# Four waits of a fused attention, FFN and mixture-of-experts kernel moved; pair rows laid side by side and the final sums dealt one block later

## The reference, cut to what matters

```python
def _L0_xattn_ref(inputs_q, inputs_kv, Wq, bq, Wk, bk, Wv, bv, Wo, bo):   # H, HD = 16, 64
    q = einsum('bqm,mhd->bqhd', inputs_q, Wq) + bq
    k = einsum('bkm,mhd->bkhd', inputs_kv, Wk) + bk
    v = einsum('bkm,mhd->bkhd', inputs_kv, Wv) + bv
    attn = softmax(einsum('bqhd,bkhd->bhqk', q / sqrt(HD), k))
    return einsum('bqhd,hdm->bqm', einsum('bhqk,bkhd->bqhd', attn, v), Wo) + bo

def _dense_path(x, ...):                                                  # H, hd = 16, 16
    q, k, v = x @ wq, x @ wk, x @ wv
    attn = softmax(where(causal, q k^T / sqrt(hd), -inf))
    h = x + rmsnorm(attn v @ wo, attn_norm_w)
    ffn = silu(h @ w1) * (h @ w3) @ w2
    return h + rmsnorm(ffn, ff_norm_w)

def _sparse_path(x, router_w, ew1, ew2, ew3, moe_norm_w):                 # E = 8, K = 2
    topw, topi = top_k(softmax(x @ router_w), K)
    g = silu(x @ ew1[e]) * (x @ ew3[e]);  eo = g @ ew2[e]
    return rmsnorm(sum_k topw_k * eo[topi_k], moe_norm_w)

x = x + _L0_xattn_ref(layernorm(x), ctx_1024, ...)
y = layernorm(x);  x = x + _dense_path(y, ...) + _sparse_path(y, ...)
```

## Time and profile before

| | |
|---|---|
| median of 3 runs | 1634.62 us (1632.85 to 1635.26) |
| the profiled execution, its own time | 1636.36 us |
| its span in the trace | 1634.6 us |
| PE busy | 1439.1 us, 88% |
| DVE busy | 820.4 us, 50% |
| ACT busy | 572.3 us, 35% |
| POOL busy | 468.3 us, 29% |
| PE clock granted, mean | 0.953 |

### The profile page before, as it was taken

The page is one execution under the profiler, slowest core; times in us unless marked ns, Lnnn a source line. Parts: engine busy times, 40 slices in busy tenths (PEclk is TensorE's granted clock), DMA queues, the critical chain, the costliest instruction groups (busy, mean ns, idle before and its releaser), DMA issues.

```text
span 1634.6 us, 23062 instructions
## 1 busy us (share of the span) xinstructions
PE 1439.1 (88%) x7753; PEld 945.7 (58%) x7754; DVE 820.4 (50%) x1711; ACT 572.3 (35%) x1217; POOL 468.3 (29%) x663
## 2 busy tenths in 40 slices
PE   6887998899889987998799879988998879999976
PEld 6533566566665655566556655665565435666654
DVE  2626445743674357436643664365536713333448
ACT  2231543054215421541155115512540343333345
POOL 4312113131412132213222222322231114555533
PEclk9988899999999999999999999999999889999988
DMA  5063006000600060006000600160014423432254
GB/s 194 1 193 130 1 1 148 21 14 1 161 8 14 5 158 20 1 13 156 15 1 26 142 15 1 37 131 15 1 47 96 134 81 117 122 100 87 86 194 141
DMA packets 92314, 115.62 MB, mean 71 GB/s; under 512 B 24872, under 2 KB 66368, under 8 KB 92224
## 3 DMA queue, kind: packets, MB, share of 16 engines
q1 hardware_dynamic: 76480, 79.78, 17.5%
q10 hardware_dynamic: 9216, 16.78, 4.4%
q0 software_dynamic: 6528, 17.87, 3.1%
HBM read 70.31 MB, written 43.68 MB: 70 GB/s over the span
## 4 chain that ended last, share of the span: by engine, by line
PE 66%; DVE 12%; DMA 7%; issue 4%; ACT 4%; POOL 4%; ACTq 1%; SPq 1%; POOLq 0%; DVEq 0%
PE ps L1037 8%; PE ps L857 7%; PE ps L876 7%; DMA room<-parts_d 6%; PE ps L1001 6%; PE ps L961 5%; DVE nm L1483 4%; PE ps L947 4%; PE ps L1054 4%; PE ps L924 3%; PE ps L1011 3%; PE ps L890 2%; PE ps L813 2%; PE ps L846 2%; PE ps L981 2%
## 5 line engine op out<-in xcount | busy, mean ns | idle before, releaser
L1483 DVE TENSOR_REDUCE nm<-ps 128x2 f32<-128x256 f32 (+3 forms) x256 | 202.7, 821 | 104.5 <-PE ps L925 103.4
L1177 ACT ACTIVATE room<-ps 128x512 f32<-128x512 f32 x320 | 181.2, 598 | 163.0 <-PE ps L949 162.1
L1001 PE MATMUL ps<-hT,w 128*128 128x512 f32 x768 | 216.6, 427 | 0.0
L1011 PE MATMUL ps<-w,room 128*128 128x256 f32 x512 | 142.9, 411 | 34.5 <-DVE room L1532 34.5
L1001 PEld LDWEIGHTS ps<-hT,w 128*128 128x128 f32 x768 | 147.6, 200 | 34.6 <-DVE hT L1511 2.0
L924 PE MATMUL ps<-room 96*128 96x128 bf16 (+3 forms) x512 | 127.6, 311 | 45.0 <-DVE nm L1483 16.3
L1201 ACT ACTIVATE room<-ps 128x512 f32<-128x512 f32 x64 | 37.5, 597 | 339.0 <-PE ps L1001 339.0
L1037 PE MATMUL ps<-room 128*128 x288 | 139.0, 605 | 1.7 <-ACT room L1231 1.7
L947 PE MATMUL ps<-room 99*128 99x384 bf16 (+3 forms) x512 | 130.6, 313 | 6.5 <-ACT room L1177 5.5
L876 PE MATMUL ps<-room 128*128 128x256 f32 x512 | 124.9, 388 | 1.9 <-ACT room L1138 1.8
L1011 PEld LDWEIGHTS ps<-w,room 128*128 128x128 f32 x512 | 94.2, 201 | 54.0 <-DVE room L1532 40.1
(11 more groups left out here) (231 smaller groups left out, 2441.0 us busy)
## 6 DMA issues: line engine op xcount, KB each, us to landing
room<-parts_d SPq DMA_DIRECT2D x48, 256.0 KB, 8.3
room<-parts_d ACTq DMA_DIRECT2D x48, 256.0 KB, 9.2
room<-xs_d SPq DMA_DIRECT2D x72, 128.5 KB, 2.1
parts_d<-room SPq DMA_DIRECT2D x64, 128.0 KB, 1.8
room<-pair_d SPq DMA_DIRECT2D x8, 1024.0 KB, 7.2
room<-in_L_ffn_ew SPq DMA_DIRECT2D x24, 256.0 KB, 5.0
xin<-in_x SPq DMA_DIRECT2D x8, 512.0 KB, 9.7
parts_d<-xnT SPq DMA_DIRECT2D x32, 128.0 KB, 1.8
```

Source lines behind the costliest of these rows:

```text
L1001: last = mm(bank(up_banks(b, m)[i]), w[:, x, k, m * P:(m + 1) * P], hT[:, y, k, :], start=((x, y, k) == terms[0]), stop=((x, y, k) == term ...
L1011: last = mm(bank((6, 7)[half], D, t % 2 * D), gT[:, m % 2, t * P:(t + 1) * P], w2[:, m, :], start=(m == 0 and t % 2 == 0), stop=(m == FB - ...
L1177: done(fn(prob[:, u * 512:(u + 1) * 512], bank(6 + n % 2), ACT.Exp), "b_exp")
L1483: done(v.tensor_reduce(nm[:, t, 2 * hp:2 * hp + 2], pair_ps, AX.X, ALU.max, negate=True), "a_max")
```

## The change

- **Bias copy.** From walk 1 on POOL makes the `bq_bc` of the next batch in a new step `nx_bq`, one block of the FFN before the end of the walk. The copies for batches 0 and 1 stay in `x_turn`.
- **Key products by halves.** m 0 and m 1 wait for 31 of the 32 maxima, m 2 and m 3 for all.
- **q loads.** ACT issues the six loads of `rep_q` at the head of its step `v` (0), ahead of the copy for the scatter; there it waits for the six stores of the queries.
- **First shifts.** PE's `shift` (0) moves from block 6's start, ahead of `max` 16, to behind `max` 19; it waits until `max` 18 is reduced, and `max` 20 instead of `max` 16 waits for `mT`. `nx_stats` moves from the end of block 5 to that of block 6 and `nx_apply` from the end of block 6 to that of block 7.
- **Pair rows.** The row of token (b, t, p) and choice k in `pair_d` becomes ((b·128 + p)·4 + t)·2 + k. A partition of a pair load then reads 8 KB in a row instead of four pieces of 2 KB.
- **Final sums.** In `ending()` the `gate` and `mix` of a batch come one FFN block later than before, behind the `fd` steps, and `mix_sq` and `mix_y` two blocks after the gate's own number.

```diff
 for _m in range(3, FB):
-    STEPS += [("fu", _m, 0)] + ([("shift", 0)] if _m == 6 else []) + _max[:1] + [("fg", _m, 0), ("fu", _m, 1)] + _max[1:2]
-    STEPS += [("fg", _m, 1), ("fd", _m - 1, 0)] + _max[2:4] + [("fd", _m - 1, 1)] + _max[4:(5 if _m < 5 else 6)]
-    STEPS += {5: [("shift_parts", 0), ("nx_stats",)], 6: [("nx_apply",)]}.get(_m, [])
+    STEPS += [("fu", _m, 0)] + _max[:1] + [("fg", _m, 0), ("fu", _m, 1)] + _max[1:2]
+    STEPS += [("fg", _m, 1), ("fd", _m - 1, 0)] + _max[2:4] + ([("shift", 0)] if _m == 6 else []) + [("fd", _m - 1, 1)] + _max[4:(5 if _m < 5 else 6)]
+    STEPS += {5: [("shift_parts", 0)], 6: [("nx_stats",)], 7: [("nx_bq",), ("nx_apply",)]}.get(_m, [])
     _max = _max[(5 if _m < 5 else 6):]
...
 def ending():
     for m in range(FB + 1):
         if m < FB:
-            order += [("fu", m, 0), ("fu", m, 1), ("gate", m), ("mix", m), ("fg", m, 0), ("fg", m, 1)]
-        if m:
-            order += [("fd", m - 1, 0), ("fd", m - 1, 1), ("mix_sq", m - 1), ("mix_y", m - 1)]
+            order += [("fu", m, 0), ("fu", m, 1), ("fg", m, 0), ("fg", m, 1)]
+        if m >= 1:
+            order += [("fd", m - 1, 0), ("fd", m - 1, 1), ("gate", m - 1), ("mix", m - 1)]
+        if m >= 2:
+            order += [("mix_sq", m - 2), ("mix_y", m - 2)]
+    order += [("mix_sq", B - 1), ("mix_y", B - 1)]
...
-            pairs_v = pair_d[0:2 * B * S, :].rearrange("(b t p k) d -> b p t (k d)", b=B, t=T, k=2)
+            pairs_v = pair_d[0:2 * B * S, :].rearrange("(b p t k) d -> b p t (k d)", b=B, t=T, k=2)
...
-                                              (E + 1, [[P, E + 1]], 2 * B * S, 1), (2 * B * T, [[2 * P, B * T], [1, 2]], 0, 2)):
+                                              (E + 1, [[P, E + 1]], 2 * B * S, 1), (2 * B * T, [[2 * S, B], [2, T], [1, 2]], 0, 2 * T)):
...
-                    elif step[0] == "x_turn":
+                    elif step[0] == "x_turn" and (c is None or c == 0):
...
+                    elif step[0] == "nx_bq" and b > 0:
+                        need(pool, b, "pT_ps", 2 * T)
+                        need(pool, b, "scat", per["scat"])
+                        carry_wait(2)
+                        done(g.tensor_copy(bq_bc, bq[:, :].unsqueeze(2).to_broadcast([P, PAIRS, P])), "bq")
...
-                            if c is not None:
-                                need(pe, c, "a_max", per["a_max"])
+                        if c is not None and half == 0:
+                            need(pe, c, "a_max", per["a_max"] - 1 + k)
...
-                        if nmax == 16:
+                        if nmax == 20:
                             need(pe, b, "mT_sb", 1)
...
                         need(pe, (b, c)[i], "m_part", i + 1)
+                        if i == 0:
+                            need(pe, b, "a_max", 19)
...
                     elif kind == "v":
                         t = step[1]
                         if t == 0:
+                            if c is not None:
+                                need(act, c, "b_ps", per["b_ps"])
+                            need(act, b, "q_out", per["q_out"])
+                            for j in range(NREP):
+                                src = parts_d[Q_PART[j], 0, :, :, :].rearrange("(h d) a n -> d h (a n)", d=HD)
+                                done(act.dma_start(q_rep[j:KREP:NREP, :, :].rearrange("d (h a) n -> d h (a n)", a=KD), src), "rep_q", 16)
...
                         done(fn(g_b, g_a, ACT.Exp), "gexp")
-                        if c is not None:
-                            need(act, c, "b_ps", per["b_ps"])
-                        need(act, b, "q_out", per["q_out"])
-                        for j in range(NREP):
-                            src = parts_d[Q_PART[j], 0, :, :, :].rearrange("(h d) a n -> d h (a n)", d=HD)
-                            done(act.dma_start(q_rep[j:KREP:NREP, :, :].rearrange("d (h a) n -> d h (a n)", a=KD), src), "rep_q", 16)
```

## The result

| | before | after |
|---|---|---|
| median of 4 runs | 1634.94 us (1632.85 to 1641.13) | 1586.86 us (1586.43 to 1587.05) |
| ratio | | 0.9699, 95% interval 0.9673 to 0.9726 |
| span in the trace | 1634.6 us | 1584.7 us |
| PE clock granted, mean | 0.953 | 0.962 |

The account below looks back on a forecast made before the run. The prediction took PE's work plus its waits, and the slow clock behind them, to bound the kernel, with DVE deciding the maxima and ending. Terms -24.6 - 3.5 - 21.9 + 4.5 + 3.5 + 0 - 3.7 + 0 = -45.7 gave 1589 us, range 1574 to 1606.

Parts of the forecast that it names:

- the three waits of the earlier trace: PE's waits before the change: POOL's bias copy 14.7 us, query and key loads 13.8, DVE's copy to mT 12.7.
- First shifts, -28.1: Split to last maximum: DVE decides, its idle falls from 5.2 to 1.1 us; -24.6 in six walks, -3.5 in walk 7.
- Bias copy, -21.9: PE's bqk at walk starts: the 14.7 us wait for POOL goes, and -7.2 of slow clock behind it.
- Halves, +4.5: Key products: no earlier m 2, but PE's gaps merge to 1.8 us; clock falls in half of six walks, 1.5 us each.
- m 2 starts when it would have: Key products: x_turn's second half waits for DVE's bank 1 copy anyway, so starting m 0 and m 1 earlier gains 0.
- q loads, +3.5: FFN start to max 0: ACT held 4.4 us, tanh and data waits go; net +0.5 a walk, seven walks.
- the 21 that I had named as a sign of being wrong: Sign of error: max 0 over 21 us behind the first FFN matmul's old place.
- a rival at +3 a walk, with 0.22: The q loads cost what they hide: ACT's 4.4 us stay on the path, +21 instead of +3.5, 1606 us; chance 0.22.
- after every wait of over 2.5 us seen here: Premise for q loads: the clock falls again behind the 4.4 us wait, so the work ends at 1081.3, not 1079.5.
- my bound of 1.8: Key stores sharing DMA engines with the query loads would land up to 1.8 us later, holding the key loads behind them.
- Walk 0, ending, pair rows: Three terms: walk 0 at 0 (-3 to +4), ending -3.7 (-5.5 to 0), pair rows 0 (-2 to +2).
- Another wait takes its place: Rival: bqk starts early but PE then waits for exponentials or POOL's sums; half of 21.9 lost, 1600 us; chance 0.1.

Follow-up runs that it names:

- second trace of the changed kernel: The changed kernel without further edits, run in a second series on another chip; that series gave 0.9698 (0.9679 to 0.9717) against the kernel before.

## Why the prediction was right, and where it wasn't

The total was off by 2 us in the median, and by 4 between the two traces (-49.9 instead of -45.7 us). That it came so near is luck in part: the q loads cost 7 us more than forecast, and the stretch of the bias copy and the halves gave 10 us more, and the two nearly cancelled.

- **What bounds the kernel.** Right for two of the three waits of the earlier trace rows: those for POOL and for mT were on the path, and so was the clock behind them. The wait for data was on it too, but taken away alone it brought nothing (1.0012), since ACT's hold put another wait in its place.
- **First shifts, -28.1.** The table has -26.1. Undone alone it was 18.5, because the price holds a part that isn't fixed: 2.3 us a walk for the order and up to 1.6 for the clock. Right in its mechanism; that DVE decides fits its 18.68 us busy of 20.35 (I had 1.1 us idle, it is 1.7).
- **Bias copy, -21.9.** The mechanism was right, and undone alone it cost 22.7.
- **Halves, +4.5.** Wrong: the cost didn't come. The gap of 1.8 us did (0.44, then 1.64), but the clock behind it was 1.00 in walks 2 to 7 of the changed kernel. Beside the other changes it is even the old order that loses clock: with m 0 waiting for all maxima, 1.57 us in one piece, it fell in the same six walks, while in the kernel before it had been 1.00 there in walks 3 to 7. "m 2 starts when it would have" holds only as long as the clock stays up.
- **The two together.** The table's first row is -27.1 and not -17.4. Of the 9.7 us between them 4.5 are the term for the halves, 2.9 lie in walks 2 to 7 (24.8 us against the 21.9 of the bias copy), and 2.3 in walk 1, where the bias copy didn't move and for which I had nothing. What gave these 2.3 isn't shown; in the second trace of the changed kernel they are 1.2.
- **q loads, +3.5.** This step failed by its size. The hold of 4.4 us, the wait for hT and the end of the data's wait came as worked out; the clock behind the wait cost more than the 1.8 us that I took from the earlier trace rows, 2.9 us in the first 6.2 alone. Max 0 came 21.0 us behind the first FFN matmul's old place, just over the 21 that I had named as a sign of being wrong. The table has +10.3, undoing gives 11. I had weighed this as a rival at +3 a walk, with 0.22. It was that rival's mechanism at half its price, with the gain of the clock elsewhere hiding it in the total. My premise that the clock falls "after every wait of over 2.5 us seen here" was a misreading: the wait of 2.57 us for the first tanh of walk 7 (1229.91) left it at 1.00. Behind the 4.4 us for hT it was 0.50 in all seven walks. The Trainium skill says in TensorE: Matmul & The Clock Gate, section What's actually happening, that the slow clock is the default which activity releases; these seven rows agree with it.
- **Later key stores.** SP issued its key loads 1.4 us after the end of its last store before the change (1063.23 in walk 6), and 5.6 us after it in the changed kernel (1031.94). SP's wait in between is for the landing of the stores. That is 4.2 us more, and more than twice my bound of 1.8. It cost nothing here, since max 0 waits for the row numbers (0.38 us) and no longer for the data. The Trainium skill says in DMA: Bandwidth & Descriptors, section Queues, rings and completion order, that a DMA engine takes turns between the queues that have work; the trace agrees in the direction, stores beside loads of another queue land later.
- **Walk 0, ending, pair rows.** Walk 0 has -1.3 for 0, and the second trace of the changed kernel +0.8, so it is none. From the last maximum of walk 7 on it is -5.7 for -3.7: 3.4 behind the first gate, 0.9 between the last scatter and that gate (0.5 to 0.7 of it by the pair rows undone), 1.4 ahead of them.
- **"Another wait takes its place".** It did, but for the q loads and not for the bias copy.

The effects of undoing each edit alone add up to 22.7 + 18.5 + 1 + 1 + 4.4 - 11 = 37 us, and the change brought 49. Each has an uncertainty of some 4 to 6 us, and the falls of the clock don't add (in walks 1 to 6 the wait for mT lost clock five times before the change, three times with the shifts back, never with the q loads alone). How much of the 12 us is the one and how much the other stays open.

## What to carry to other kernels

Six loads issued in a row held ACT's work behind them for 3.87 us here, 0.64 us each; issued where ACT stood idle anyway, they cost it nothing. So put a DMA's issue where the engine would stand anyway, and deal a batch of loads to several such places rather than move it in one piece. When a wait for data is removed by starting the transfer earlier, count what the issuing engine then does late, and for whom. A wait of PE costs itself and what the clock loses behind it, and the second part can differ from walk to walk with the same wait, so single undone edits need not sum to the whole. A total that doesn't change can hide two stretches that do, as with the halves: compare the traces by stretches before an edit is taken to be worth nothing.

## What the runs showed of the hardware

- **The clock behind a wait isn't set by the wait alone.** In the 3 us behind it: after 4.3 to 4.4 us for hT 0.50 in all seven walks of the changed kernel; after 3.4 to 5.1 us for data 0.50 in all seven with the loads on SP; after 2.57 to 3.25 us with the loads back 0.66 to 0.70. But 1.57 us ahead of m 0 brought 0.52 to 0.58 in six walks with the halves back, where 1.72 us at that place in the kernel before had left 1.00 at the start of walks 3 to 7; in the run with the loads dealt out 2.32 and 2.36 us left it at 1.00 and 2.19 us brought 0.54; and the same 1.72 us for mT left 1.00 in one walk and 0.50 to 0.71 in five of the kernel before, 1.00 in all six with the q loads alone.
- **An issue of a DMA can lie beside the engine's own copy**: 1001.38 to 1002.00 beside 1001.42 to 1002.03 on ACT.
- **Twelve loads of 256 KB take 17 to 18 us from the first issue to the matmul that waits**, from one queue or from two (walk 6: 16.8, 17.3, 17.4, 17.6; 17.9 with the first ones beside the stores), and 20.0 us with the last stores queued between them.
